# Attention with four score bank pairs for its first batch, slot rounds with two tiles scaled on ScalarE and a tanh gate, and blending scores as rows

## The reference, cut to what matters

```python
# layer 0 (hypergraph); H: 1024 nodes x 64 edges
agg  = einsum('ben,bnf->bef', softmax over nodes of an edge, h)
beta = sigmoid((h @ a_gn)[:, None, :] + (agg @ a_ge)[:, :, None])
all_he = elu(beta[..., None] * h[:, None] + (1.0 - beta[..., None]) * agg[:, :, None])
coefs1 = softmax(where(H > 0, tanh(elu(agg) @ fcW + fcb) @ av, NEG))
g = einsum('bne,benf->bnf', coefs1, all_he)
industry = (adj / deg) @ (x @ W_ind)
pair = stack([industry, g])
coefs2 = softmax(tanh(pair @ fcW + fcb) @ av, over the two)
out = coefs2[0] * industry + coefs2[1] * g
# layer 1 (graph attention)
e = leaky_relu(e1[:, :, None] + e2[:, None, :], 0.2)
att = softmax(where(adj > 0, e, NEG))
out = elu(att @ Wh)
```

## Time and profile before

| | us |
|---|---|
| median of 3 runs | 2270.8 |
| lowest, highest | 2267.96, 2271.24 |
| profiled execution | 2270.87 |
| its span in the trace | 2269.2 |
| PE busy in it | 2044.1 |
| DVE busy in it | 2021.4 |
| ACT busy in it | 1420.8 |
| POOL busy in it | 926.4 |

### The profile page before, as it was taken

One profiled execution on the slowest core, in us unless ns is written; L12 is line 12 of the kernel. 1 busy time (PEld: TensorE's weight loads), 2 busy tenths in 40 slices (PEclk: granted clock), 3 DMA queues, 4 the chain that ended last, 5 costly groups with the idle time before them and its releaser, 6 DMA issues. The chain is left out here.

```text
span 2269.2 us, 61376 instructions
## 1 busy us (share of the span) xinstructions
PE 2044.1 (90%) x26430; PEld 1350.7 (60%) x26430; DVE 2021.4 (89%) x2705; ACT 1420.8 (63%) x2236; POOL 926.4 (41%) x532
## 2 busy tenths in 40 slices
PE   5888878578788899999999999999999999998886
PEld 5655445345576566666666666666666666665554
DVE  7578876499666999999999999999999999999995
ACT  4422234489734676667766776666766667676774
POOL 2259960136400344444444444444544444432211
PEclk9999986588988999999999999999999999999998
DMA  3000000434311221211211211210210210124442
GB/s 128 1 1 0 0 0 1 91 61 68 47 25 47 49 39 39 53 35 39 44 35 40 53 33 32 53 44 30 46 42 30 58 39 21 35 58 66 72 67 48
DMA packets 176818, 94.73 MB, mean 42 GB/s; under 512 B 158552, under 2 KB 163864, under 8 KB 176432
## 3 DMA queue, kind: packets, MB, share of 16 engines
q1 hardware_dynamic: 176560, 90.94, 18.6%
HBM read 80.09 MB, written 10.83 MB: 40 GB/s over the span
## 5 line engine op out<-in xcount | busy, mean ns | idle before, releaser
L523 ACT ACTIVATE x_sb<-x_sb,hid_neg_max 128x1024 f32<-128x1024 f32 x576 | 661.7, 1154 | 287.1 <-DVE hid_neg_max L437 286.8
L446 DVE STREAM_TRANSPOSE hid_weights_t<-x_sb 128x1024 f32<-128x1024 f32 x576 | 711.9, 1236 | 1.6 <-ACT x_sb L523 1.2
L437 DVE CUSTOM_DVE_ANT_0 x_sb<-ps_score,adj_mask,row_scale 128x1024 f32<-128x1024 f32 x512 | 638.6, 1247 | 7.3 <-PE ps_score L312 6.1
L332 PE MATMUL ps_low<-hid_weights_t,hid_x_rep 32*64 32x256 f32 x18432 | 575.5, 383 | 10.0 <-ACT hid_share L553 9.6
L312 PE MATMUL ps_score<-hid_y_hi,hid_xs 128*128 128x512 f32 x1152 | 522.1, 453 | 33.4 <-DVE hid_neg_max L437 30.4
L332 PEld LDWEIGHTS ps_low<-hid_weights_t,hid_x_rep 32*64 32x64 f32 x18432 | 392.1, 132 | 167.7 <-issue 96.7
L312 PE MATMUL ps_score<-hid_y_lo,hid_xs 128*128 128x512 f32 x1152 | 456.3, 396 | 0.0
L629 POOL TENSOR_TENSOR hid_z<-hid_z,hid_inv_cols 128x1024 f32<-128x1024 f32 x64 | 194.6, 3041 | 552.3 <-ACT hid_z L531 552.3
L312 PEld LDWEIGHTS ps_score<-hid_y_hi,hid_xs 128*128 128x128 f32 x1152 | 217.0, 188 | 259.1 <-issue 153.3
L312 PEld LDWEIGHTS ps_score<-hid_y_lo,hid_xs 128*128 128x128 f32 x1152 | 218.5, 190 | 44.5 <-issue 15.0
L621 POOL TENSOR_TENSOR hid_y_wide<-hid_y_wide,hid_y_hi 128x1024 f32<-128x1024 f32 x63 | 151.2, 2400 | 185.1 <-ACT hid_y_wide L514 185.1
(11 more groups left out here) (367 smaller groups left out, 3054.9 us busy)
## 6 DMA issues: line engine op xcount, KB each, us to landing
hid_inv_cols<-hid_inv_rows SPq DMA_DIRECT2D x64, 512.0 KB, 3.8
hid_x_rep<-hid_row_space SPq DMA_DIRECT2D x64, 256.0 KB, 5.8
gat_x_rep<-gat_row_space SPq DMA_DIRECT2D x32, 256.0 KB, 5.4
gat_e_wide<-gat_e_space SPq DMA_DIRECT2D x8, 512.0 KB, 6.5
marks<-hid_mark_rows SPq DMA_DIRECT2D x8, 512.0 KB, 4.9
x_sb<-in_x SPq DMA_DIRECT2D x4, 512.0 KB, 5.7
hyp_neighbours<-in_adj SPq DMA_DIRECT2D x4, 512.0 KB, 6.9
edge_adj_high<-in_adj SPq DMA_DIRECT2D x4, 512.0 KB, 9.1
```

Of the source, the lines that this page charges most:

```text
L332: ins = pe.matmul(m.ps_low[c * F:(c + 1) * F, a, 0:NT * Q], x_rep[a * Q:(a + 1) * Q, batch_of(g) % 2, b, :], weights_t[a * Q:(a + 1) * Q, ...
L437: dve.tensor_tensor_reduce(ring[:, i % RING, :], m.ps_score[:, i % 2, :], mask, scale, HUGE, ALU.add, ALU.min, neg_max[:, g % 2, t:t + 1]) ...
L446: dve.transpose(weights_t[:, g % 2, :, t, :], ring[:, i % RING, :].rearrange("p (b j) -> p b j", j=Q)).then_inc(tile_turned, 1)
L523: act.activation(ring[:, i % RING, :], ring[:, i % RING, :], ACT.Exp, scale=-1.0, bias=neg_max[:, g % 2, t:t + 1], accum_out=row_sum[:, g ...
```

## The change

Five things change.

1. Graph attention: in batch 0 the tiles take turns over four bank pairs (two in `ps_score`, two in `ps_low`), so three pairs are opened ahead of the first add_row. From batch 1 on it is as before.
2. Slot rounds: the gate is tanh(v/2) + 1, one table function on ScalarE; the "+ 1" sits in scale_away, and the factor 1/2 in `half_ident`, by which add_diff multiplies. L2268 and L2269 go. `rank` is no longer lowered; a counter `slot_no` (128x1) is raised instead and compared with. The coefficient's min-and-mask step moves behind scale_away(1).
3. The shares of tiles 2 and 5 are multiplied by ScalarE, in two halves of four 128x64 copies with a scale, behind the exponentials of tiles 3 and 4, and of 6 and 7. GpSimd multiplies the other six and adds in the order 0, 1, 3, 2, 4, 6, 5, 7.
4. All eight tiles of `h` are divided in the blending block.
5. Blending scores: `av`, repeated over 32 columns, is now the weight, and the difference moves as 512 columns, four matmuls into four groups of 32 partitions of one bank. ScalarE's exponential is then 128x512, four transposes bring the scores back to columns, and VectorE reads those. find_hidden of the second pair moves ahead of turn("n", 2).

```diff
+        def score_bank(i):
+            if i < NT and i % 4 >= 2:
+                lo = i % 4 * 2 - 4
+                return m.ps_low[:, lo:lo + 2, :].rearrange("p a n -> p (a n)")
+            return m.ps_score[:, i % 2, :]
+
+        def last_user(i):
+            return i - 4 if i < NT + 2 else i - 2
+
...
             def open_banks(i):
-                if i >= 2:
-                    pe.wait_ge(masked_ready, i - 1)
+                if i == 2:
+                    pe.wait_ge(e2_taken, 1)
+                if last_user(i) >= 0:
+                    pe.wait_ge(masked_ready, last_user(i) + 1)
                 for half in range(2):
                     cols = slice(half * HALF, (half + 1) * HALF)
-                    ins = pe.matmul(m.ps_score[:, i % 2, cols], pick[:, 0, :], m.adj_t[:, 0, cols],
+                    ins = pe.matmul(score_bank(i)[:, cols], pick[:, 0, :], m.adj_t[:, 0, cols],
...
-            for i in range(2):
+            for i in range(3):
                 open_banks(i)
             for i in range(3):
                 add_row(i)
-                if i == 0:
-                    open_banks(2)
...
+            BY_ACT = (2, 5)
+            ADD_ORDER = (0, 1, 3, 2, 4, 6, 5, 7)
+
+            def place(t):
+                return ADD_ORDER.index(t) + 1
...
                     def add_diff(t):
                         pe.wait_ge(diff_ready, k * NT + t + 1)
-                        pe.matmul(row_banks(t)[0], m.ident[:], diff[:, t % 2, :], start=False,
+                        pe.matmul(row_banks(t)[0], half_ident[:], diff[:, t % 2, :], start=False,
...
                     act.wait_ge(beta_asked, k + 1)
-                    act.activation(beta[:], beta[:], ACT.Exp, scale=-1.0).then_inc(beta_exped, 1)
+                    act.activation(beta[:], beta[:], ACT.Tanh, scale=0.5).then_inc(beta_bent, 1)
                     act.wait_ge(coef_asked, k + 1)
                     act.activation(coef[:], coef[:], ACT.Exp).then_inc(coef_exped, 1)
+
+                    def scale_half(n, h):
+                        t = BY_ACT[n]
+                        act.wait_ge(share_ready, k * NT + t + 1)
+                        act.wait_ge(coef_taken, k + 2)
+                        for b in range(4 * h, 4 * h + 4):
+                            s = share[:, t % 4, b * F:(b + 1) * F]
+                            ins = act.activation(s, s, ACT.Copy, scale=pool_coef[:, t, b:b + 1])
+                        if h:
+                            ins.then_inc(act_scaled, 1)
+
                     for t in range(NT):
                         act.wait_ge(blend_ready, k * NT + t + 1)
                         act.activation(blend_exp[:, t % 2, :], row_banks(t)[0], ACT.Exp,
                                        bias=minus_one[:, 0:1]).then_inc(blend_exped, 1)
+                        if t in (3, 4):
+                            scale_half(0, t - 3)
+                        if t in (6, 7):
+                            scale_half(1, t - 6)
...
-                    for t in range(NT):
-                        pool.wait_ge(share_ready, k * NT + t + 1)
+                    own = 0
+                    for t in ADD_ORDER:
                         s = share[:, t % 4, :]
-                        pool.tensor_tensor(by_batch(s), by_batch(s), along(pool_coef, t), ALU.mult)\
-                            .then_inc(scaled, 1)
-                        pool.wait_ge(scaled, k * NT + t + 1)
+                        if t in BY_ACT:
+                            pool.wait_ge(act_scaled, k * len(BY_ACT) + BY_ACT.index(t) + 1)
+                        else:
+                            own += 1
+                            pool.wait_ge(share_ready, k * NT + t + 1)
+                            pool.tensor_tensor(by_batch(s), by_batch(s), along(pool_coef, t), ALU.mult)\
+                                .then_inc(scaled, 1)
+                            pool.wait_ge(scaled, k * (NT - len(BY_ACT)) + own)
                         pool.tensor_tensor(rows[:, t, :], rows[:, t, :], s, ALU.add)\
                             .then_inc(share_added, 1)
...
+                dve.memset(slot_no[:], 0.0).then_inc(step, 1)
+                dve.tensor_scalar(half_ident[:], m.ident[:], 0.5, None, ALU.mult).then_inc(halved, 1)
...
                     link(dve.tensor_tensor(coef[:], small[:, :, 0:B], best[:], ALU.subtract))
-                    dve.scalar_tensor_tensor(out=coef[:], in0=coef[:], scalar=0.0,
-                                             in1=linked[:].unsqueeze(2).to_broadcast([P, NT, B]),
-                                             op0=ALU.min, op1=ALU.mult).then_inc(coef_asked, 1)
-                    dve.wait_ge(beta_exped, k + 1)
-                    link(dve.tensor_scalar(beta[:], beta[:], 1.0, None, ALU.add))
-                    link(dve.reciprocal(beta[:], beta[:]))
-
                     def scale_away(t):
                         dve.wait_ge(rows_ready, k * NT + t + 1)
                         if t >= 2:
                             dve.wait_ge(blend_ready, k * NT + t - 1)
-                        dve.tensor_tensor(by_batch(diff[:, t % 2, :]), by_batch(row_banks(t)[1]),
-                                          along(beta, t), ALU.mult).then_inc(diff_ready, 1)
+                        dve.scalar_tensor_tensor(out=by_batch(diff[:, t % 2, :]), in0=along(beta, t), scalar=1.0,
+                                                 in1=by_batch(row_banks(t)[1]), op0=ALU.add,
+                                                 op1=ALU.mult).then_inc(diff_ready, 1)
...
+                    dve.wait_ge(beta_bent, k + 1)
                     scale_away(0)
                     scale_away(1)
+                    dve.scalar_tensor_tensor(out=coef[:], in0=coef[:], scalar=0.0,
+                                             in1=linked[:].unsqueeze(2).to_broadcast([P, NT, B]),
+                                             op0=ALU.min, op1=ALU.mult).then_inc(coef_asked, 1)
+                    link(dve.tensor_scalar(slot_no[:], slot_no[:], 1.0, None, ALU.add))
...
-                    link(dve.tensor_scalar(rank[:], rank[:], -1.0, None, ALU.add))
...
-                            dve.tensor_scalar(pick[:], rank[:], 0.0, None, ALU.is_equal)\
+                            dve.tensor_scalar(pick[:], rank[:], slot_no[:, 0:1], None, ALU.is_equal)\
                                .then_inc(picked, 1)
...
-                dve.wait_ge(inverted, 1)
-                dve.wait_ge(share_added, count * NT + 1)
-                for t in range(SCALED):
-                    row = m.h[:, t, :, :]
-                    dve.tensor_tensor(row, row, along(coef_sum, t), ALU.mult)
...
+        score_rows = m.ps_low[:, 3, :]
+        score_cols = m.ps_low[:, 2, :].rearrange("p (t k c r) -> p c t k r", t=4, k=2, c=2)[:, :, :, :, 0]
...
-                    for t in range(NT):
-                        ins = pe.matmul(score_bank(q)[:, 2 * t + k:2 * t + k + 1], apart[:, k, t * P:(t + 1) * P],
-                                        av[:], start=True, stop=True)
+                    for c in range(2):
+                        row = (2 * k + c) * 32
+                        ins = pe.matmul(score_rows[row:row + 32, :], av[:].to_broadcast([P, 32]),
+                                        apart[:, k, half(c)], start=True, stop=True)
                     ins.then_inc(scored, 1)
+
+            def turn_scores(q):
+                pe.wait_ge(exped, q + 1)
+                if q:
+                    pe.wait_ge(score_taken, q)
+                for t in range(4):
+                    ins = pe.transpose(m.ps_low[:, 2, t * P:(t + 1) * P], score_exp[:, t * P:(t + 1) * P], m.ident[:])
+                ins.then_inc(score_turned, 1)
...
             def exp_scores(q):
                 act.wait_ge(scored, 2 * q + 2)
-                act.activation(first[:, q, :, :], score_bank(q).rearrange("p (t k) -> p t k", k=2), ACT.Exp,
-                               scale=-1.0).then_inc(exped, 1)
+                if q:
+                    act.wait_ge(score_turned, q)
+                act.activation(score_exp[:], score_rows, ACT.Exp, scale=-1.0).then_inc(exped, 1)
...
             def blend(q):
                 f, x, n = first[:, q, :, :], pair(m.x, q), pair(neighbours, q)
-                dve.wait_ge(exped, q + 1)
-                link(dve.tensor_scalar(f, f, 1.0, None, ALU.add))
+                dve.wait_ge(score_turned, q + 1)
+                dve.tensor_scalar(f.rearrange("p (c t) k -> p c t k", c=2), score_cols, 1.0, None, ALU.add)\
+                   .then_inc(score_taken, 1)
+                dve.wait_ge(score_taken, q + 1)
```

42 lines of the change are left out of this document (24 added, 18 removed).

## The result

The changed kernel takes 2251.97 us (median; 2248.69 to 2252.57), the kernel before, run beside it, 2270.89: ratio 0.9919, 95% interval 0.9903 to 0.9935. That is 18.9 us less, where 11.55 were forecast.

| stage | forecast | measured | from |
|---|---|---|---|
| set-up and slot rounds | -5.8 | -12.3 | last share 314.55, now 302.26 |
| end of the rounds | +0.75 | +1.0 | to VectorE's first division in blending |
| division of h | +0.7 | +0.7 | to the first turn |
| blending scores | -4.2 | -7.1 | to add_row(0): 435.14, now 417.43 |
| first attention batch | -3.0 | -2.7 | to the mask of tile 8: 460.52, now 440.15 |

A forecast was written before the change was run, and what follows sets the result against it. No engine was taken as saturated; chains crossing engines bound the kernel. Terms 0.2 - 6.0 + 0.75 + 0.7 - 4.2 - 3.0 = -11.55 took 2270.87 to 2259.3 us; eight-in-ten range 2252 to 2267, own range 2254.5 to 2263.5.

The forecast's parts named there:

- Slot rounds: Slot rounds: share 0 comes 0.72 us sooner in eight rounds, 0.2 in the first; -6.0 us, ends 0 and -8.0.
- PE is the floor: Slot rounds: add_diff(0) stands behind twelve row-pair matmuls, so the exponential stays at 177.53; at most 0.89 us a round.
- VectorE's step waits for the end of GpSimd's instruction: Slot rounds: coefficient and `rank` steps end with GpSimd's add, 0.09 and 0.56 us behind it.
- rival (a): Slot rounds: GpSimd's last add still ends near 177.9 and holds VectorE every round; price 6.0, 2265.3 us; chance 0.14.
- wrong as a whole if GpSimd's slack stays 0.7 us: Slot rounds: sign that the whole forecast is wrong; GpSimd had 0.71 us of slack per round.
- ScalarE's copies: Slot rounds: four 128x64 copies take 0.93 us, fit the 1.10 to 1.14 us gap between exponentials; 0.
- rival (c): Slot rounds: ScalarE's copies don't fit, delaying exponentials of tiles 4, 5, 7; 15.7 us, 2275; chance 0.08.
- End of the rounds, division: Last round's end: ScalarE's tile 5 copies add +0.75 us; blending: the longer first division of h adds +0.7.
- Blending scores: Blending: column groups run in pairs, saving 10.2 us, less exponentials 2.0 and transposes 4.0; net -4.2, ends -7 and +3.
- rival (b): Blending scores: the column groups run one after the other; +1 instead of -4.2, 2264.5 us; chance 0.08.
- First attention batch: Graph attention, batch 0: the 3.28 us a tile PE ring stays, only the late start goes; -3.0 us, ends -1 and -8.
- Rival (d): First attention batch: four pairs free it from PE's ring, VectorE sets 2.5 us a tile; 2255.3 us; chance 0.10.

The follow-up runs named there:

- Experiment 2: Kernel before with three more 128x512 matmuls per slot round on TensorE, ahead of the first row pair; 2273.77 us, ratio 1.0018.
- experiment 1: Changed kernel with three more 128x512 matmuls per slot round on TensorE, ahead of the first row pair; 2254.85 us, ratio 0.992.
- Experiment 4: Changed kernel with the 128x1024 step on `rank` restored in place of the 128x1 counter; 2253.5 us, ratio 0.9923.
- Experiment 9: Changed kernel with early opens in the first attention batch and the division of h as in the kernel before; 2243.23 us, ratio 0.9867.
- experiment 7: Changed kernel with PE's list reordered in the first attention batch: banks of tile i + 4 opened ahead of add_row(i + 3); 2245.52 us, ratio 0.988.

## Why the prediction was right or wrong

**Slot rounds (-6.0, measured -12.5 without the set-up).** The mis-sized term. The order of the limits was right where a round starts at 1.2 GHz: GpSimd's last add ends 1.5 us sooner (1.4 forecast), the coefficient's step in the two slow-start rounds ends 0.08 us behind it, and the share comes 0.83 and 0.93 us sooner (0.72 forecast, 0.89 called the most to be had). The failed step is "so PE is the floor, the exponential cannot come sooner than 177.53": most of the twelve matmuls of that floor ran at the half clock. From the first of them to add_diff(0) it is 4.45 us in the third round of before and 2.90 in that of after, and six of eight rounds had the short one. Then the exponential starts at 3.4 us instead of 4.9, and the next limit is GpSimd's last add. Experiment 2 shows that this clock was worth nothing before, experiment 1 that it is worth 1.0 us a round now. That the time still fell into the range is luck: nothing in the sum stands for a change of clock at the rounds' start. Which round gets it is not settled: PE idles 0.5 us ahead of the row pairs in the rounds of before and 0.76 in the rounds of after, those with a slow start too, so it is not that gap alone.

**GpSimd and the late steps.** That VectorE's step waits for the end of GpSimd's instruction held where GpSimd was first. Experiment 4 shows the reverse: rank starts 0.07 us ahead of GpSimd's add, takes 0.68 us, and the add takes 1.73 instead of 1.27. By that GpSimd's last add ends 0.46 us later, the running sum is held to its end (0.80 us instead of 0.58), and this is the 0.45 us that rank costs. The condition of rival (a), a last add as late as before, did not occur, but its mechanism sets the first share of every full-clock round, by the running sum and not by the coefficient's step. The sign "wrong as a whole if GpSimd's slack stays 0.7 us" came true in the letter (GpSimd still waits 0.71 us for the first share of the third round) and was a bad sign: that wait follows the share wherever it lies, and GpSimd's work of a round fell from 19.2 to 16.8 us. The Trainium skill ("GPSIMD Engine Reference", section 1, Specifications) has the two engines in contention for their SBUF interfaces; the traces agree, in both directions.

**ScalarE's copies.** Four take 1.05 us, not 0.93, and the exponential of tile 7 now holds its share 0.66 us (0.26 before); rival (c) asked for 0.38 us a copy, and it is 0.26. The round's shorter `pick` step (0.76 us for 1.17) makes up for it. The gaps ahead of the exponentials of tiles 4, 5 and 7 are 0.15 to 0.19 us, as forecast.

**End of the rounds, division.** Right: +1.0 and +0.7 for +0.75 and +0.7. (2.67 times 0.49 is 1.31 and not 1.2; one took 1.22.) Experiment 9 shows a place where the division is free, in a wait that I had named.

**Blending scores (-4.2, about -5 over all traces, -7.1 in the pair).** Near in sum by luck, from wrong parts. Two matmuls were taken to run at once: eight records were to last 2.0 us at full clock and lasted 1.06. They are four matmuls, 0.85 us each alone and 3.4 one after the other, so all four column groups ran together and rival (b) is out. The Trainium skill ("TensorE: Matmul & The Clock Gate", Part 3, packing small matmuls) gives 2.38 times for three groups; the trace has 3.2 times (3.4 by 1.06 us) for four. But the saving was counted as if the score were the last thing the exponential waits for. At full clock it is ScalarE itself, in the kernel before too (4.39 us behind the score's start, directly behind a table load), so 2 x 1.8 was not saved there. Two sums beside this one are off: pairs at 1.6 times instead of 2 make the net -1.7 and not -2.8, and rival (b) has +1 where the range has +3 for the same case.

**First attention batch (-3.0, measured -2.7; -2.9 over all traces).** Right, ring and pace included. add_row(3) came 4.99 us behind add_row(0), for 5.06 forecast. Rival (d) did not occur, and experiment 7 made it occur by order alone, at 2.28 us a tile.

**What comes later "only moves with it".** Not quite: 1.4 us went to a lower grant in equal code, by chance of the execution.

## What to carry to other kernels

A floor worked out from rows at the half clock is not a floor: say at which clock each term was measured, give the sum at either, and name the limit that comes next when the floor falls. More buffers help only if the list of the engine that fills them is reordered to use them. Before a shorter step is counted, look whether the instruction that waits for it is also behind others on its own engine.

## What the runs showed of the hardware

- At full clock four 32-column groups of a 512-column fp32 matmul took 1.06 us together (after); one full-array matmul takes 0.85.
- The 128x1024 step on `rank` and a GpSimd add that overlap cost the one that starts second: 1.66 us for 0.69 when GpSimd was first (before), 1.73 for 1.27 when VectorE was (experiment 4). The shares and `scale_away`, which take one input from PSUM, kept their 0.69 us beside GpSimd.
- A 128x64 running sum on VectorE took 0.58 us for 0.23 and ended 0.08 us behind the end of GpSimd's add, in every full-clock round of after.
- Three more matmuls a round ahead of the row pairs turned the starts of all eight rounds behind the first from 1.2 to 2.4 GHz in the kernel before (experiment 2), and the round stayed at 20.56 us.
